# VectorE writes the second tile's X1l ahead of the inverse's blocks, and the blocks' compact form stays in PSUM

## What is computed

```python
def step(carry, kvq):                      # once per token, in order
    W, b = carry
    k, v, q = kvq                          # k = theta_K x, v = theta_V x, q = theta_Q x
    pred = W @ k + b
    g = 2.0 / d_h * (pred - v)
    W = W - LR * jnp.outer(g, k)
    b = b - LR * g
    return (W, b), W @ q + b
...
x = _layernorm(x + attn(x))
x = _layernorm(x + ffn(x))
```

## Time and profile before

| | us |
|---|---|
| three runs, median (lowest to highest) | 2301.88 (2300.41 to 2303.6) |
| profiled execution, its own time | 2296.03 |
| its span | 2294.2 |
| PE busy in the span | 2193.5 (96%) |
| DVE busy | 1548.6 (68%) |
| POOL busy | 1225.2 (53%) |
| ACT busy | 891.7 (39%) |

### The profile page before, as it was taken

How to read it: one execution, slowest core, us unless ns; L and a number is a source line. 1 busy time by engine, 2 the same in 40 slices (tenths; PEclk the granted TensorE clock), 3 DMA queues, 4 the chain that set the end, 5 groups by cost and what they waited for, 6 DMA issues and landing times.

```text
span 2294.2 us, 40089 instructions
## 1 busy us (share of the span) xinstructions
PE 2193.5 (96%) x12834; PEld 1899.8 (83%) x12834; DVE 1548.6 (68%) x3666; ACT 891.7 (39%) x1943; POOL 1225.2 (53%) x1168
## 2 busy tenths in 40 slices
PE   7999999999999999999999999999889999999896
PEld 6888888888888888888888888888779998998775
DVE  5666666666566778666656667775546545898798
ACT  4333333333333333333333334232255555555444
POOL 1344444433444333755544554346457777777777
PEclk9999999999999999999999999999989999999998
DMA  4211212122211111112211111110564435997996
GB/s 172 74 65 65 74 65 83 65 76 82 74 65 65 40 45 37 55 65 78 80 46 38 37 47 38 39 37 20 223 232 139 145 114 188 305 305 247 314 330 216
DMA packets 112201, 257.18 MB, mean 112 GB/s; under 512 B 21618, under 2 KB 23282, under 8 KB 109056
## 3 DMA queue, kind: packets, MB, share of 16 engines
q1 hardware_dynamic: 83776, 187.35, 23.5%
q0 software_dynamic: 27936, 67.22, 8.8%
q10 hardware_dynamic: 288, 0.04, 0.0%
HBM read 160.36 MB, written 105.26 MB: 116 GB/s over the span
## 4 chain that ended last, share of the span: by engine, by line
PE 77%; DVE 13%; issue 4%; POOL 2%; DMA 2%; ACT 1%; DVEq 0%; SPq 0%; POOLq 0%; ACTq 0%
PE banks L115 23%; PE banks L116 22%; PE banks L117 22%; PE banks L121 4%; DVE xc L1118 3%; PE banks L762 2%; PE banks L503 1%; PE banks L789 1%; DVE W L1115 1%; DVE b_Y L1118 1%; DVE banks L1115 1%; PE banks L541 1%; DVE X1l L1115 1%; DVE b_small L1661 1%; DMA W<-wd 1%
## 5 line engine op out<-in xcount | busy, mean ns | idle before, releaser
L115 PE MATMUL banks<-W 128*128 128x512 f32 (+1 forms) x2040 | 752.5, 369 | 10.8 <-DVE W L1115 7.6
L117 PE MATMUL banks<-W 128*128 128x512 f32 (+1 forms) x2040 | 718.0, 352 | 0.0
L116 PE MATMUL banks<-W 128*128 128x512 f32 (+1 forms) x2040 | 716.9, 351 | 0.0
L115 PEld LDWEIGHTS banks<-W 128*128 128x128 f32 x2040 | 387.9, 190 | 59.8 <-DVE W L1115 7.6
L117 PEld LDWEIGHTS banks<-W 128*128 128x128 f32 x2040 | 386.8, 190 | 54.8
L116 PEld LDWEIGHTS banks<-W 128*128 128x128 f32 x2040 | 388.3, 190 | 46.9
L1718 POOL TENSOR_TENSOR W<-S,W 128x512 fp32r<-128x512 f32 (+1 forms) x249 | 326.3, 1337 | 134.8 <-ACT W L833 134.2
L833 ACT ACTIVATE W<-banks 128x512 fp32r<-128x512 f32 x320 | 191.0, 598 | 503.3 <-DVE banks L1115 232.7
L1718 POOL TENSOR_TENSOR X<-X,B 128x1024 f32<-128x1024 f32 x32 | 76.8, 2401 | 459.0 <-DMA X<-in_x 459.0
L833 ACT ACTIVATE W<-S 128x512 fp32r<-128x512 f32 (+1 forms) x256 | 161.7, 653 | 219.5 <-DVE S L1115 213.2
L1115 DVE TENSOR_TENSOR W<-banks,W 128x512 fp32r<-128x512 f32 x192 | 132.4, 690 | 139.3 <-ACT W L833 139.2
(11 more groups left out here) (164 smaller groups left out, 4414.2 us busy)
## 6 DMA issues: line engine op xcount, KB each, us to landing
RG<-ys SPq DMA_DIRECT2D x128, 256.0 KB, 4.0
XT<-in_xT SPq DMA_DIRECT2D x32, 512.0 KB, 3.6
X<-in_x SPq DMA_DIRECT2D x32, 512.0 KB, 3.5
x1d<-X SPq DMA_DIRECT2D x64, 256.0 KB, 2.1
wd<-RG SPq DMA_DIRECT2D x32, 512.0 KB, 3.9
W<-wd SPq DMA_DIRECT2D x16, 1024.0 KB, 12.6
out<-b_Y SPq DMA_DIRECT2D x64, 256.0 KB, 4.4
zd<-X SPq DMA_DIRECT2D x52, 256.0 KB, 2.0
```

Of the source, the lines that this page charges most:

```text
L115: e.matmul(o, ll, rh, start=start, stop=False, skip_group_check=True)
L116: e.matmul(o, lh, rl, start=False, stop=False, skip_group_check=True)
L117: return e.matmul(o, lh, rh, start=False, stop=stop, skip_group_check=True)
```

## The change

It has two parts, both in DVE's program.

- In the loop, `turn_x1(t - 1, 1)` (X1l of the second tile) moves from behind `inv_m(t)` and the second half of `p_part(t, 0)` to ahead of `inv_m(t)`.
- In `scores(t)`, `rows_of(1)` and `rows_of(2)` move ahead of the reduction, behind `rows_of(0)`, and the semaphore counts after the last of the three. The reduction writes the compact form gd over the products in the bank A, which the three have read by then, and no longer to SBUF; the two instructions that write R read it from PSUM. PE's `inv_t` for n = 1 and 2 waits for the same count as for n = 0.

```diff
@@ -320,7 +320,7 @@
-        k.xc, k.gd, k.rw = sb("xc", [NB, BS]), sb("gd", [NB, BS]), sb("rw", [KC, E])
+        k.xc, k.rw = sb("xc", [NB, BS]), sb("rw", [KC, E])
@@ -543,7 +543,7 @@
     def inv_t(t, n):
         o = bank(w, ("T", t, n), k.s_T1, NL * t + n + 1)
-        w.wait_ge(k.s_sc, 4 * t + (4 if n else 2))
+        w.wait_ge(k.s_sc, 4 * t + 2)
@@ -1148,8 +1148,10 @@
         stt(k.T1[:], g, 1.0, mBD.unsqueeze(1).to_broadcast(bc), ALU.add, ALU.mult).then_inc(k.s_sc, 1)
-        rows_of(0).then_inc(k.s_sc, 1)
-        gd = k.gd[:]
+        for n in range(NL):
+            z = rows_of(n)
+        z.then_inc(k.s_sc, 1)
+        gd = g[:, :, 0:BS]
         w.wait_ge(k.s_sc, 4 * t + 2)
         e.tensor_reduce(gd, k.T1[:].rearrange("p b (k j) -> p b j k", k=NBL), AX.X, ALU.add).then_inc(k.s_sc, 1)
@@ -1159,8 +1161,6 @@
             tt(o, gd[:, :, h * HS:BS].unsqueeze(1).to_broadcast(rows), own.to_broadcast(rows), ALU.mult).then_inc(k.s_R, 1)
-        rows_of(1)
-        rows_of(2)
         w.wait_ge(k.s_R, 2 * t + 2)
         stt(kq, kq, -1.0, mAT, ALU.add, ALU.mult).then_inc(k.s_sc, 1)
@@ -1524,10 +1524,11 @@
         next(first)
         for _ in columns:
             pass
+        if t > 0:
+            turn_x1(t - 1, 1)
         inv_m(t)
         next(first, None)
         if t > 0:
-            turn_x1(t - 1, 1)
             logits(t - 1, 0)
         next(second)
         next(second, None)
```

## The result

The changed kernel takes 2264.53 us (median of four runs, 2263.81 to 2267.36); the kernel before, beside it on the same chip, 2302.74 (2300.41 to 2308.31). The ratio is 0.9833, with a 95% interval from 0.9813 to 0.9853: faster by 1.7%. The profiled execution is one of the four: 2264.78 us, span 2263.0, against 2296.03 and 2294.2 of before. So the medians differ by 38.2 us and the profiled executions by 31.25.

What follows compares the result with a forecast made beforehand. PE, busy 96%, was taken to be bound by its waits for X1l. The terms 14.0 + 7.7 + 2.8 + 4.6 + 2.4 = 31.5 us gave 2264.5 for the profiled execution, 2270.4 for the median; range 2264 to 2284.

Steps and rivals of the forecast that it cites:

- What bounds the kernel: PE at line 115 waits 27.6 us for DVE's X1l, late because POOL holds the blocks' instruction ahead of it.
- Part 1, late steps: Steps 18 to 26: moving X1l ahead of the blocks removes PE's wait in full, 7.7 us.
- The term of steps 15 to 17: X1l wait of 3.0 us goes, less 0.2 as PE waits for M0 in step 15: 2.8 us.
- Part 1, early steps: Steps 2 to 14: moving X1l ahead of the blocks removes PE's wait in full, 14.0 us.
- the margin of 0.14 to 0.21: Late steps: time M0 still has to spare, in us, when PE comes 0.87 earlier and Pf 0.6 to 0.67 earlier.
- Part 2: R read from PSUM is not held by POOL, at the free price; bounds -1.5 and +0.1 us a step.
- Step 0: PE's first wait of 3.37 us goes, the second, for the blocks, may grow: gain 2.4, between 0 and 4.24.
- After the loop: From step 31 on: later waits counted at nothing; the experts' weight loads move with the loop and pass all gain on.
- The median: Profiled execution taken as 5.9 us under the median for the changed kernel too: 2301.9 - 31.5 = 2270.4.
- more than forecast: Rival, 10%: steps with routing each give another 1.1 to 1.5 us from R's hold; total gain 36, giving 2266.
- the slower rival: Rival, 5%: POOL starts a long instruction before the blocks, M0 comes late, 0.4 us a step longer: +9, giving 2311.
- X1l is held too: Rival, 5%: POOL holds X1l as it does the blocks, and M0 eats PE's gain: within 0.2%, about 2300.

Runs made afterwards that it cites:

- The run with the short residual: Kernel before, with POOL's X<-X,brows cut to one column of 512, which leaves out the bias on the other 511: 2275.5 us, ratio 0.988.
- M0 first on ACT: Changed kernel, with ACT writing M0 of the first level ahead of the silu, HH and HF of the previous step's tiles: 2265.41 us, ratio 0.984.
- part 2 alone: Kernel before, with only the compact form gd in PSUM and the rows moved earlier; X1l stays behind the blocks: 2278.48 us, ratio 0.989.
- part 1 alone: Kernel before, with only X1l moved ahead of the blocks' instruction; gd and R stay in SBUF: 2275.73 us, ratio 0.9876.
- the second profile: Changed kernel timed and profiled again without edit, beside the kernel before: 2264.14 us, ratio 0.9832, span 2261.6.
- the third profile: Changed kernel measured once more without edit, beside the version with M0 earlier on ACT and step 0 freed from POOL: 2264.36 us, ratio 0.9841.
- The second profile, nearer to the median: Kernel before, profiled again without edit: 2304.82 us, span 2303.0, 8.8 over its first profile.

## Why the prediction was right, and where it was not

**What bounds the kernel: right.** PE's wait for X1l was the one thing, POOL's hold of a DVE instruction its cause. The run with the short residual shows this by itself.

**Part 1, late steps: right to 0.1 us, by two errors that cancel.** 7.7 forecast, 7.7 measured; X1l unheld at 0.68; the blocks end 0.29 behind POOL as before; M0 ends 0.62 earlier against the mixture, as worked out. The term of steps 15 to 17 held too, by its reason: in step 15 the wait for X1l went and PE waited 1.70 for M0 in place of 0.81.

**Part 1, early steps: the term was 3.2 us too small.** 14.0 was the sum of the waits as the profile gives them, in 12 steps. The leads show that each wait was 0.24 longer than its row. PE in step 2, before (first two rows) and after:

```profile
140.06 0.38 PE L617 MATMUL banks<-ident,HF 128*128 128x128 f32 x2
141.61 0.36 PE L115 MATMUL banks<-WS,X1l 128*128 128x264 f32 x1 [1.16 <-DVE X1l L1115]
```

```profile
139.23 0.38 PE L617 MATMUL banks<-ident,HF 128*128 128x128 f32 x2
139.37 0.37 PE L115 MATMUL banks<-WS,X1l 128*128 128x264 f32 x1
```

From start to start it was 1.55 and is 0.14: 1.41 gained where the row says 1.16. The end of a matmul is modelled, and its 0.38 us hides the rest, as the next one can start 0.14 after it. Twelve times 0.24 is 2.9; step 11, which showed no wait, gave 0.26 all the same. The late steps had the same 0.24 (1.11 where the earlier trace rows has 0.87). It used up the margin of 0.14 to 0.21 that the prediction had left for M0, so PE waits for M0 there (1107.97 in the rows of step 21) and 0.14 to 0.2 a step go back. Two small errors cancel in the 7.7, which is luck. With M0 first on ACT these 0.2 a step came back.

**Part 2: the price was right, its use was undersized.** R takes 0.62 us from PSUM where it took 0.63 from SBUF. Step 0 of the changed kernel, DVE and POOL:

```profile
29.52 0.62 DVE L1115 TENSOR_TENSOR MM<-banks,smallc 128x256 f32<-128x256 f32 x2
...
31.47 1.97 DVE L1508 COPY xc<-smallc 128x2 f32<-128x2 f32 x1
...
28.80 4.62 POOL L1719 TENSOR_TENSOR W<-S,W 128x2048 fp32r<-128x2048 f32 x1 [27.95 <-ACT W L833]
```

That is not the 65 ns more a piece that the prediction had estimated from the table in "The TRN2 errata" of the Trainium skill (VectorE: DVE Perf Modes); here the measurement decides. The prediction saw that POOL's work would move 1.5 us forward with R (1.4 measured) and "should be over" when the blocks ask. It didn't count that this alone takes the wait out of the early steps, as part 2 alone shows, and that M0, which takes 0.5 us a step back in part 1 alone, then doesn't.

**Step 0: 2.4 forecast; 0.8, 1.3 and 2.5 in three profiles. The path was right, the clock behind it was left out.** The first wait of 3.37 went. The copy into xc, in the rows above, was held from 31.47 to 33.44, two hundredths behind POOL's end at 33.42. This is the rule that the prediction cited and set beside its sum: by the Trainium skill (SBUF — State Buffer, "Who interferes with whom") a copy within SBUF can take the port pair that DVE shares with GpSimd. The row agrees, for a copy of two elements a partition. PE came to the blocks at 38.77 and not 38.2 (PE's timeline, and the stretch around it):

```profile
38.77 0.44 PE L541 MATMUL banks<-ident,MM 128*128 128x128 f32 x2 [2.13 <-DVE MM L1115]
```

```profile
38.00:42.00 4.00, 3.23 (x12) 2.62 (x13) 2.78 (x7) 0.77 (x2) 0.10 (x1) 0.70 0.94 198
```

The 0.6 are no error of the path: POOL's W<-S,W began 0.56 later in this execution (28.80; 28.24 in the earlier trace rows). In the second profile it began at 28.24 again, and PE came at 38.23, as forecast. What the forecast lacked is the clock: behind that wait of 2.13 it was 0.70 here and 0.57 there (38 to 42), and the next turn on PE, 5.40 behind this one in before, came 6.47 behind it both times. 2.4 less these 1.1 is the 1.3 of the second profile, and less 0.56 the 0.8 of the first. In the third profile the wait was 1.68 and the clock 1.00, and the forecast's gain is there.

**After the loop: forecast 0, measured -2.2.** The load that ended the chain took 16.45 us in the first profile of before, 17.54, 18.05 and 17.83 in three of the changed kernel, and 16.83 to 23.63 in the seven others whose chain has it. This scatters between executions, and the forecast had no term for it; it is 1.1 of the 2.2, and the rest stays open. So the sum, 31.5 against 31.2 measured in the profiles, is better than its terms: 3.2 too little in the early steps stand against 1.6 too much in step 0 and 2.2 lost after the loop. That they cancel is luck.

**The median: 5.9 us too high, and this step was wrong.** The prediction took the profiled execution's place under the median (5.9) as something that the changed kernel's would have too. It was not. That execution had fewer of the very waits that were to go (steps 1 and 11) and full clock in step 0. The second profile, nearer to the median, has two more waits (2.3 us), and the lower clock behind those of steps 0 and 29 (1.4 and 1.5). The change removes these waits, so against the median it gains 38 us, and 31 against the first profile. In that one profile this makes 5.2 of the 6.7 us; its later start (1.5) and what it lost after the loop (2.6) are nothing that the change removes. How often each of these comes in other executions of before wasn't seen, so how the 6.7 are made up is likely, not shown. The range, 2264 to 2284, held the median by half a microsecond. The rival "more than forecast" gave 2266, but by another mechanism (R's hold in the steps with routing), and steps 15 to 17 show no such gain. Neither the slower rival nor "X1l is held too" left a trace: X1l takes 0.68 in every step.

## What to carry to other kernels

When a DVE instruction has a duration that varies, look at POOL's timeline: if it ends a fixed time (0.3 us here) behind POOL's end, it is held. Move one whose inputs include PSUM in front of it, or get one of its inputs from PSUM. Read what a wait costs from start to start of the two matmuls around it, not from the idle time. And before you set a forecast against a median, ask what makes the profiled execution shorter than it: where that is the thing that you remove, the offset goes with it.

## What the runs showed of the hardware

- A copy of 128x2 within SBUF, 0.16 us alone, took 1.97 beside POOL's instruction and ended 0.02 behind its end (1.40 to 1.97, and 0.02 to 0.04 behind, in five profiles); the blocks' instruction ends 0.29 behind it, R's pair in step 0 ended 0.48 behind.
- After waits of PE of 3.43 and 3.48 us in step 0 the granted clock fell (0.50 to 0.77 in the 7 us behind), after 3.37 and 2.99 (the short residual) it didn't; after 2.13 it did twice of twice (0.70 and 0.57 from 38 to 42), after 1.95, 1.68 and 1.56 it didn't. In step 16 it fell after 2.18, three times of three after 2.6 (0.66, 0.83, 0.83) and once of four after 1.8. In later steps of before it fell behind 1.43 and 1.41 (step 27) and once behind 0.78 (step 29); with the short residual it didn't fall behind 1.42 in step 27. So the length of the wait doesn't decide alone; what else does wasn't tried.
- The same weight load took 16.45 to 23.63 us in eleven profiles. Two edits that each remove a wait of PE were worth nothing that can be told alone: the clock and this load scatter by as much as they bring.
